# Layer norms of an eight-stage transformer kernel: ScalarE instead of VectorE writes the normalised tiles

## The reference, cut to what matters

```python
def _layernorm(x, axis=-1, eps=1e-05):
    m = jnp.mean(x, axis=axis, keepdims=True)
    v = jnp.var(x, axis=axis, keepdims=True)
    return (x - m) / jnp.sqrt(v + eps)

x = x + attention_a0(_layernorm(x))     # 1: rotary attention, causal
x = x + ffn_f0(_layernorm(x))           # 2: 1 of 4 experts per row
x = x + keyed_sum_b0(_layernorm(x))     # 3
x = x + ffn_f0(_layernorm(x))           # 4
x = x + linear_attention_a1(_layernorm(x))  # 5
x = x + ffn_f1(_layernorm(x))           # 6: 2 of 8 experts per row
x = x + attention_b1(_layernorm(x))     # 7
x = x + ffn_f1(_layernorm(x))           # 8
```

## Time and profile before

| what | value |
|---|---|
| median of 3 runs | 2225.22 us (2221.39 to 2228.47) |
| the profiled execution | 2220.95 us, its span in the trace 2219.1 us |
| busy share of the span | PE 82%, DVE 52%, PEld 46%, ACT 33%, POOL 22% |
| DMA | 123 MB, 56 GB/s on average |

### The profile page before, as it was taken

The page is one execution under the profiler, slowest core; times in us unless marked ns, Lnnn a source line. Parts: engine busy times, 40 slices in busy tenths (PEclk is TensorE's granted clock), DMA queues, the critical chain, the costliest instruction groups (busy, mean ns, idle before and its releaser), DMA issues.

```text
span 2219.1 us, 32673 instructions
## 1 busy us (share of the span) xinstructions
PE 1817.6 (82%) x10328; PEld 1016.5 (46%) x10329; DVE 1150.6 (52%) x2341; ACT 722.2 (33%) x1396; POOL 494.1 (22%) x840
## 2 busy tenths in 40 slices
PE   6699999998489994757999497699467999976992
PEld 4344444432356663544666355376243444344761
DVE  7688888872412215751122456143376887462423
ACT  2277777765111110111111101022023667610220
POOL 2222222221300005621000500500441222133022
PEclk9599999997799996868999698799786999987996
DMA  3331111122200002001000310223223211002322
GB/s 97 83 124 41 42 41 39 38 95 106 81 26 24 19 21 90 1 22 35 24 24 21 116 52 3 88 93 101 66 62 73 37 34 24 1 27 80 99 91 80
DMA packets 97291, 123.35 MB, mean 56 GB/s; under 512 B 19704, under 2 KB 77976, under 8 KB 96408
## 3 DMA queue, kind: packets, MB, share of 16 engines
q1 hardware_dynamic: 87960, 96.67, 15.0%
q0 software_dynamic: 9216, 25.18, 3.5%
HBM read 78.35 MB, written 42.86 MB: 55 GB/s over the span
## 4 chain that ended last, share of the span: by engine, by line
PE 68%; DVE 13%; issue 9%; another core or an unknown queue 4%; POOL 3%; DMA 2%; ACT 1%; SPq 0%; POOLq 0%; DVEq 0%; ACTq 0%
PE psum L1331 12%; PE psum L981 9%; PE psum L965 7%; PE psum L1352 6%; PE psum L929 6%; DVE region_a L778 5%; PE psum L1566 5%; PE psum L1538 3%; PE psum L347 2%; POOL y_norm L1226 2%; PE psum L1769 2%; PE psum L1584 2%; PE psum L1585 2%; PE psum L1341 1%
## 5 line engine op out<-in xcount | busy, mean ns | idle before, releaser
L778 DVE TENSOR_REDUCE region_a<-psum 128x1 f32<-128x640 f32 (+7 forms) x576 | 527.9, 953 | 94.5 <-PE psum L934 54.6
L866 ACT ACTIVATE region_w<-psum 128x512 f32<-128x512 f32 x864 | 465.7, 600 | 227.1 <-PE psum L965 223.7
L1331 PE MATMUL psum<-region_w,region_a 128*128 x608 | 271.9, 601 | 1.5 <-DVE region_a L1407 1.2
L981 PE MATMUL psum<-region_w,region_a 128*32 128x512 f32 (+3 forms) x2304 | 256.6, 520 | 0.8 <-POOL region_w L681 0.6
L929 PE MATMUL psum<-region_a,y_norm 48*128 48x512 bf16 (+7 forms) x816 | 226.2, 354 | 27.4 <-DVE region_a L778 14.3
L681 POOL TENSOR_SCALAR_AFFINE_SELECT region_w<-region_w 128x512 f32<-128x512 f32 x192 | 121.8, 635 | 462.1 <-ACT region_w L866 457.7
L1226 POOL DMA_INDIRECT y_norm<-result_rows,region_a x64 | 63.0, 985 | 713.9 <-DMA result_rows<-region_a 695.9
L965 PE MATMUL psum<-y_norm,region_a 51*128 51x512 bf16 (+1 forms) x612 | 205.7, 400 | 5.9 <-DMA y_norm<-region_a 4.0
L1331 PEld LDWEIGHTS psum<-region_w,region_a 128*128 128x128 f32 x608 | 114.3, 193 | 132.5 <-issue 132.5
L1414 DVE TENSOR_TENSOR region_a<-psum,region_a 128x512 f32<-128x512 f32 x76 | 52.6, 692 | 215.8 <-PE psum L1331 215.8
L1538 PE MATMUL psum<-y_t,region_w 128*128 128x512 f32 (+1 forms) x192 | 100.1, 676 | 73.9 <-DVE ctx L1657 53.3
(11 more groups left out here) (186 smaller groups left out, 2607.4 us busy)
## 6 DMA issues: line engine op xcount, KB each, us to landing
region_a<-sorted_rows SPq DMA_DIRECT2D x116, 128.0 KB, 2.0
result_rows<-region_a SPq DMA_DIRECT2D x116, 128.0 KB, 1.7
y_norm<-a_q SPq DMA_DIRECT2D x132, 64.0 KB
sorted_rows<-ctx SPq DMA_DIRECT2D x1, 4992.0 KB, 17.2
y_norm<-b_q SPq DMA_DIRECT2D x36, 128.0 KB
region_w<-in_f_wg SPq DMA_DIRECT2D x1, 4096.0 KB, 13.3
region_w<-in_f_wu SPq DMA_DIRECT2D x1, 4096.0 KB, 12.9
region_w<-in_f_wd SPq DMA_DIRECT2D x1, 4096.0 KB, 14.2
```

The source lines that it names most:

```text
L778: dve.tensor_reduce(dst, src, AX_X, ALU.max, negate=True).then_inc(self.ring_done.sem, 1)
L866: act.activation(self.p[col % P_RING][:, :, i % 4, :], c.bank[ST_BANKS[s % 3]].rearrange("p (h t) -> p h t", h=GQ), ACT.Exp, scale=self.sc ...
L981: mm = pe.matmul(c.bank[ACC_BANK][32 * h:32 * h + 32, P * lo:512], self.vp[slot][:, j, :], self.p[col % P_RING][:, h, lo:4, :], start=(j = ...
L1331: mm = pe.matmul(bank[:, :], self.yt[:, f, :], w[:, f, bass.ds(own * self.hidden + 512 * half, 512)], start=(f == 0), stop=(f == FT - 1))
```

## The change

ACT writes the normalised tiles with one `activation` each, Identity(x * scale + bias), where scale is rstd and bias a new per-row value shift = -mean * rstd. DVE makes the four shifts of a group with one `scalar_tensor_tensor` on 128x4 in the place where the four `tensor_scalar` stood. In ACT's order the four activations of group g stand before the copy L308 of group g and behind the copy of group g-1. The copies of the second half stay on DVE.

```diff
@@ class LayerNorm
+        self.shift = c.shared_sem("ln_shift_set")
@@ def vector
-        def normalize(g):
+        def shifts(g):
+            s = slice(4 * g, 4 * g + 4)
             dve.wait_ge(self.rstd, NG * k + g + 1)
-            for t in range(4 * g, 4 * g + 4):
-                dve.tensor_scalar(c.yn[:, t, :], c.x[:, t, :], c.mv[:, t, 0:1], c.rstd[:, t:t + 1],
-                                  ALU.subtract, ALU.mult).then_inc(self.norm, 1)
+            dve.scalar_tensor_tensor(out=c.shift[:, s], in0=c.mv[:, s, 0], scalar=-1.0, in1=c.rstd[:, s], op0=ALU.mult,
+                                     op1=ALU.mult).then_inc(self.shift, 1)
@@ for g in range(NG + 2)
             if 1 <= g <= NG:
-                normalize(g - 1)
+                shifts(g - 1)
@@ def scalar
         for g in range(NG):
+            act.wait_ge(self.shift, NG * k + g + 1)
+            for t in range(4 * g, 4 * g + 4):
+                act.activation(c.yn[:, t, :], c.x[:, t, :], ACT.Identity, bias=c.shift[:, t:t + 1],
+                               scale=c.rstd[:, t:t + 1]).then_inc(self.norm, 1)
             act.wait_ge(self.turned, FT * (NG * k + g) + 1)
             act.activation(c.yt[:, 0, 512 * g:512 * g + 512], c.bank[4 + 2 * (g % 2)][:, :],
                            ACT.Copy).then_inc(self.yt0, 1)
```

More of the change, by code:

```diff
@@ L89, in __init__ @@
         self.rstd = self.sb("ln_rstd", [P, NT], F32)
+        self.shift = self.sb("ln_shift", [P, NT], F32)
         self.vareps = self.sb("ln_vareps", [P, NT], F32)
```

## The result

The changed kernel takes 2241.29 us (median of five, 2240.84 to 2249.73) and the kernel before, timed beside it, 2226.23 (2221.39 to 2228.47). The ratio is 1.0083 with a 95% interval of 1.0066 to 1.01: slower, 15 us, where 19 were forecast. The profiled execution took 2241.29, its span is 2239.4, so against the profiled execution of before it is 20.3 us longer.

What follows compares the result with a forecast made beforehand. The prediction took DVE to be the busiest engine in the norms and ACT's new cycle to cost more: 3.9 (norm 1) + 10.2 + 4.8 = 18.9 us, giving 2239.9 against the profiled execution, 2244 on the median; range 2234 to 2254.

Steps and rivals of the forecast that it cites:

- What bounds a norm: In the norms DVE is busiest and on the path; a microsecond before the last transposes is one for the kernel.
- ACT's round through PE and back: In each norm ACT normalises four tiles, waits for PE's transposes, copies, then starts the next group: N + T = 3.74 us.
- the ring: The cycle in each group: ACT's normalisations, PE's transposes, ACT's copy, and only then the next group's normalisations.
- N: Time of ACT's four normalisations of a group: 2.04 us, one taking 584 ns; ends 1.25 and 2.34.
- T: Time from ACT's last normalisation of a group to its next one, through PE's transposes and ACT's copy: 1.70 us, low end 1.19.
- The shift: DVE's making of a group's four shifts, on the way to the normalisations: 0.16 us, 0.2 with the hand-off to ACT.
- Norms 2, 4, 6, 8: Norms behind a projection: 6.02 us for 3.29 up to the last transposes, net 2.54 slower each, 10.2 in all.
- the wait of 0.20: In the projection PE waits 0.20 us for an add on DVE; with the normalisation gone from DVE this is gained.
- Norms 3, 5, 7: Gather-fed norms: 2.10, 1.61 and 2.73 us slower, less 0.56 each from earlier adds; net 4.8 in all.
- The relief of DVE: Rival: DVE's shorter steps in the norms win, about -17 us, 2208, if N + T falls under 2.1; chance 3%.
- Nothing to be seen: Rival: with operands that cost nothing and PE at its quicker level, sum near 0, 2225 us; chance 5%.
- The table loads: Rival: Identity not in the resident table, two loads of 1.28 us per norm, time 2250 to 2264; chance 4%.

Runs made afterwards that it cites:

- experiment 2: Changed kernel with ACT normalising the next group before it waits for the transposes of this one: 2222.31 us, ratio 0.9992 to the kernel before.
- experiment 5: Kernel before, plus a wait: DVE normalises a group only after ACT has copied the group ahead. 2187.81 us on another chip, ratio 1.009.
- the second trace: Kernel before, unedited, traced in one further execution: 2219.74 us, span 2217.8.
- experiment 1: Changed kernel once more, unaltered: 2245.47 us, ratio 1.0096 to the kernel before.
- experiment 10: Changed kernel a third time, unedited: 2246.26 us, ratio 1.01 to the kernel before.
- experiment 9: Changed kernel plus six transposes of the identity into an unread bank, ahead of PE's wait for the last group: 2225.84 us, ratio 1.0009 to the kernel before.
- experiment 7: Kernel before, DVE normalising all, with only DVE's copies one round later: 2155.05 us, ratio 0.9941 to the kernel before.
- experiment 8: Two tiles of each group normalised on DVE, two on ACT a group ahead of its copies, DVE's copies one round later: 2139.08 us, ratio 0.9859 to the kernel before.
- experiment 3: Changed kernel with only the per-row scale in ACT's activation, the mean not subtracted: 2235.51 us, ratio 1.0051 to the kernel before.

## Why the prediction was right, and where it was off

**What bounds a norm** held. DVE's time there was on the path, and ACT's became so. The mechanism that the prediction put first, ACT's round through PE and back, shows in the timeline at 3.76 a round against a forecast of 3.74. Experiments 2 and 5 carry it from both sides. With the ring opened and the operations kept, the loss is gone; with the ring closed and the operations kept on DVE, the loss is there. What cost most of the time is the order in which the engine must normalise, and not which engine it is. With the ring open, ACT's longer normalisations still leave the norms 2 to 3.7 us over the kernel before.

**N** was forecast at 2.04 and is 2.07. (Of its 584 ns, 16 are a choice between 0 and 20; no row gave them.) The Trainium skill (ScalarE: Activation LUTs, What ACT_TABLE_LOAD costs) has figures from which an estimate is 585 ns for one such activation and 2.06 for four; the trace now agrees for two operands (587 ns, 2.07).

**T** was 1.70 and is 1.69: 3.76 less 2.07. **The shift** was 0.16, and is 0.13 to 0.17, with one of 0.72 in norm 3 while POOL adds.

**Norms 2, 4, 6, 8**: forecast 10.2, measured 9.4. The part inside the norm was right (2.76 for 2.73). The gain, the wait of 0.20, was too small: 0.43 came back in the projection.

**Norms 3, 5, 7**: forecast 4.8, measured 1.7. This is the term that was mis-sized. The part behind the shift of group 2 was right (2.13, 1.65 and 2.77 for 2.10, 1.61 and 2.73). But the prediction took 2.78 as the time in which a gather lands, though its row gave that only as an upper bound, and with it a gain of 0.56 a norm. It landed within 2.14, and the gain was the upper end, 1.20: 1.9 of the miss of 3.1. Another 1.0 is the one gather issue of 1.91 in the trace of before on which the comparison rests (at 859.26); in the second trace it took 0.95. Against the second trace the three norms cost 2.9, and the gathers' gain is the whole miss. Whether the change removes the slow issue stays open: in norm 3 it is there in three of the four traces in which DVE normalises all tiles, and in none in which it normalises none.

**What the sum left out**: 5.2 us in the blocks. The prediction treated PE's products behind a norm as a fixed length ("a microsecond more or less before the last transposes is one for the kernel"). They are not. The mean granted clock of the whole kernel is 0.877 to 0.881 in the 16 executions of the changed kernel (the first five and those of experiments 1 and 10), and 0.881 to 0.889 in the 40 of the kernel before that ran beside experiments 1 and 10. With the ring on DVE (experiment 5) it fell as well, 0.889 to 0.894 against 0.893 to 0.897, and with ACT's ring opened (experiment 2) it is back at 0.885 to 0.893. The extra time comes in pieces of 0.2 to 2 us, block by block. They repeat in three traces of the changed kernel to within 2 us (6 in block 8), and the kernel before differs from itself by up to 3 in a block. Yet outside the norms its two traces come to 1982.1 and 1982.6 us, and the three of the changed kernel to 1987.3, 1990.9 and 1992.8. So the sign and the rough size are shown: 5 to 11 us by the traces, 4 to 8 by the medians of experiments 1 and 10 (21.1 and 22.6 us, of which the norms are 15 to 17). That the clock is behind all of it is argued from experiment 9, not shown piece by piece. Two further pieces, the expert loops of blocks 6 and 8, are 2.9 longer and 3.0 shorter between the two first traces, and cancel; they change by as much between executions of one kernel.

So a sum that was 2 to 4 too high in the norms and some 5 too low in a term that was missing came out near the truth. The forecast of 2244.0 is 2.7 over the median beside it. The mechanism and its size in the norms were foreseen; that the total came so close is luck.

**The rivals.** The relief of DVE would have needed a round of less than 2.1 us; it is 3.76. Yet experiments 7 and 8 show that there was something to gain on DVE: 0.6% from later copies, 1.4% with half of the tiles moved. "Nothing to be seen" needed operands that cost nothing; one costs 92 ns (experiment 3). The table loads didn't come: the groups by line of after show eight in all, as before, and the first now stands at the line of the new operation at 0.8 us, before anything waits for it.

## What to carry to other kernels

Before moving work to an idle engine, write out the order of that engine's program: if it does a step, waits for another engine to use it, finishes that, and only then does the next step, its whole round trip is the price of each group, however idle it looks. Put the next group's work ahead of the wait (here 23 us), and try a short burst split between both engines before giving it all to one (here 0.8%). Before calling a difference in one stage an effect, take a second trace of the kernel that nothing was changed in. And count what a pause of PE does to the products behind it, not only the pause.

## What the runs showed of the hardware that was not expected

- **Idle products pay.** Six transposes of the identity in each norm, 1.49 us of PE time that lies almost whole in its wait, took the kernel from 1.01 to 1.0009. PE went into the next product at a granted clock of 1.00 in place of 0.50, and a run of 16 products took 1.90 in place of 3.60.
- **A slow gather.** The longest of the 64 gather issues took 1.91 us in three of four traces in which DVE normalises all tiles (1.22 in the fourth), 1.58 with three of four tiles on DVE, 1.26 with two, and 1.18 to 1.25 in all with none. The Trainium skill (SBUF — State Buffer, section SBUF: two separate sides) has DVE and GpSimd take turns at a shared pair of ports. Most of these numbers go the same way, the 1.22 of the fourth trace doesn't, and no run isolates it.
- **The stage of experts varies by itself.** Between scatter and gathers it took 118.2 us in block 6 and 121.2 in block 8 of the kernel before, 121.1 and 118.2 after. In the second trace of the kernel before it is 120.8 in both, and in two more of the changed kernel 120.8 and 120.1, 121.2 and 121.2. In the first two traces DVE is busy for the same 44.6 us in all four stretches, and the granted clock is 0.94 in the first three and 0.98 in the last, so the clock alone doesn't explain it. On the other chip it is 112 to 114 in both blocks of every kernel, and from the norm on block 6 (up to the first add) is some 20 us shorter and block 8 some 33. Why stays open.
